# Attention over pooled image patches and text: queries and keys cut into their two parts before the turn, with the step's order rewritten on every engine

## The chip, the cores and the metric

The kernel runs on one core of one Trainium2 chip. The metric is the device time of one launch, in microseconds (us). The kernel before took 3253.87 us, the median of three runs (3253.17 to 3255.74).

## What is computed

The input is 64 images of 12 channels, 224 x 224, and 64 texts of 32 tokens, width 192. The reference, cut:

```python
pooled = x.reshape(64, 12, 14, 16, 14, 16).sum(axis=(3, 5))
h = concat([einsum('bcij,ce->bije', pooled, channel_weights), txt])  # 64 x 228 x 192
a = layernorm(h) * norm_scale + norm_bias
q, k, v = split(a @ W_attn + b_attn)        # 12 heads of 16, q and k rotated (RoPE)
att = softmax([sink, causal(q @ k.T / 4)])[..., 1:]
h = h + ((att @ v) @ W_proj + b_proj) * rezero
f = layernorm(h)                            # tokens to 8 experts, the top 2, with
h = h + moe(f)                              # capacity; rms norm, silu(g) * u, down
```

## The kernel before, in words

**Stages.** The first part of the kernel goes over the 64 images and ends with h (stored to `out`) and with every token's normed row, written to its two slots of `moe_rows` by indirect DMAs from GpSimd (L1272). The second part, from about 2040 us on, is the mixture of experts; it goes over tiles of 456 slots, adds into `out`, and is not touched by the change.

**The step.** The first part is a software pipeline of 68 steps. Five images are in work in one step, at five stages: `p` (folded and pooled), `a` (first norm, qkv product, rotation), `m` (scores for the row maxima), `t` (transposed scores, exponentials, attention, output), `z` (second norm, gate, routing, scatter). `batches` (L1188) makes the five; the image that is `p` in one step is `a` in the next. From the fifth step to the 64th, 60 steps, all five are there. Each engine has its own program, and its order inside a step is written out by hand: `step_tensor` (L1033), `step_scalar` (L1095), `step_vector` (L1134), `pass1_gpsimd` (L1229), `pass1_sync` (L1205). Semaphores join them; each engine runs strictly in its order.

**Precision.** Scores need more than one product of rounded numbers. Each query and key number is taken as a high part plus the rest, and the four 16-wide terms of a head stand side by side, so that one product of 64 rows a head gives the full score (`qk` is 114 tokens x 2 halves x 24 heads x 4 terms x 16). Before the change, GpSimd writes the rotated numbers four times over into `qk` in float32 (`add_rotation`, L713, four instructions of 768 elements a step). TensorE turns them (`turn_qk`, L880: six blocks T0 to T5 of four transposes each, L892). ScalarE copies a block into `rounded` with rounding (`round_qk`, L768, L775), and VectorE makes the parts while it moves the block to its place in `q_t` or `k_t` (`split_qk`, L538: two instructions of 64 partitions for a query block, L550; one of 128 for a key block, L556).

**Scores.** `score` (L895), nine blocks C0 to C8: C0 to C2 hold four heads of 114 x 114 (L904, L907), C3 to C8 two heads of 114 x 228 (L913, L915). VectorE takes the row maxima of each (`max_scores`, L561, L571), then `make_shift` (L573, L578) builds a tile `shift`, which TensorE turns (`turn_shift`, L919, L924), ScalarE rounds (`round_shift`, L777) and VectorE splits (`split_shift`, L583). `score_t` (L927), nine blocks S0 to S8, makes the scores of `t` again, transposed and with the shift taken off (L938 to L941, or L944 to L949). ScalarE takes their exponentials (`exp_scores`, L782), and `attend` (L953, three groups) multiplies with the values (L965, L967). `turn_y`, `normalize`, `turn_yn`, `copy_yn`, `project` (L996) and `residual` (L602) follow.

**Banks.** T, S and C blocks share PSUM banks 0 to 3 in turn, in the order of the list `RING`; `bank_free` (L864) waits for the reader of the block four places before. Bank 6 serves the channel sums, the first norm's turn, the qkv products and v in turn; bank 7 the second token half of the qk product, the turned shift, and all of z's routing.

**The norms.** `norm1_stats` on VectorE, `inverse_std` on GpSimd (L699; four small instructions, L705 to L711), `norm1_apply` on ScalarE, `turn_xn` on TensorE (L838), `copy_xn` on ScalarE, `make_qk` on TensorE (L841, one half of the tokens each), `rotate` on VectorE (L527: L533, L535) is the chain of an image at `a`.

**GpSimd's order before:** both `inverse_std`, three `fold_image` (L686), `add_rotation` 0, four scatters of z, `add_rotation` 1, `spread_patches` (L694).

**Routing.** `choose` (L615), `rank` (TensorE), `weigh` (L637), `assign` (L658). `hot_sum` (L635) adds two slices of `hot`, `seen` is added to twice (L677, L679); all four tensors there lie in SBUF, and `hot_sum` and `seen` are bf16.

Of the kernel before, what the change touches and what calls it, by code (L numbers as in the profile page):

```python
# [22 lines left out]
NG = CH // GRP  # L23
# [101 lines left out]
def build(nc, x, txt, chan_w, norm_scale, norm_bias, w_attn, b_attn, w_proj, b_proj, sinks,  # L125
# [17 lines left out]
    with ctx:  # L143
# [99 lines left out]
        gw = sb("gw", [TT, 2, 2])  # L243
        hot = sb("hot", [TT, 2, 2, E])
        hot_sum = sb("hot_sum", [TT, 2, E], bf16)
        seen = sb("seen", [TT, E], bf16)
# [63 lines left out]
        qk_rotated = [sem(f"qk_rotated{t}") for t in range(2)]  # L310
        qk_turned = [sem(f"qk_turned{k}") for k in range(6)]
        qk_rounded = sem("qk_rounded")
        qk_split = [sem(f"qk_split{k}") for k in range(6)]
# [109 lines left out]
        def setup_vector(dve):  # L423
# [12 lines left out]
            for tile in (w_qkv[C:C1, :, :], pieces[:, 0:2 * QF].bitcast(fp32), k_t[0][:, :, :, TT:TT + 1].bitcast(fp32), k_t[1][:, :, :, TT:TT + 1].bitcast(fp32),  # L436
                         shift[:, :, :], seen[:, :], val[0][:, :, :, :], val[1][:, :, :, :], row[0][:, :, :],
                         row[1][:, :, :]):
                nc.vector.memset(tile, 0.0)
# [40 lines left out]
        def setup_tensor(pe):  # L480
            pe.wait_ge(loaded, 16 * N_SMALL)
            for half in range(2):
# [9 lines left out]
        RING = [("score_t" if c == "S" else "turn", int(k)) for c, k in  # L492
                (item for item in "T0 T1 S0 T2 S1 S2 T3 S3 S4 T4 S5 S6 T5 S7 S8".split())]
        RING += [("score", k) for k in range(9)]
# [32 lines left out]
        def rotate(dve, at, t):  # L527
# [3 lines left out]
            wait(dve, qk_rotated[t], 2 * at.b)  # L531
            src = bank[6 + t][0:TT, 0:2 * D]
# [5 lines left out]
        def split_qk(dve, at, r):  # L538

            dve.wait_ge(qk_rounded, 6 * at.b + r + 1)  # L540
            src, hi = bank[bank_of("turn", r)], rounded[r % 2]
            k = TURNS[r]
            if r == 0:
                wait(dve, scored_t[8], at.b - 1)
            if k < 3:
                for side in range(2):
                    lo = slice(64 * side, 64 * side + 64)

                    dst = q_t[at.par][lo, :, :].rearrange("p (a s) n -> p a s n", s=2)[:, 2 * k:2 * k + 2, side, :]
                    ins = nc.vector.scalar_tensor_tensor(  # L550
                        out=dst, in0=hi[lo, :].bitcast(fp32).rearrange("p (a n) -> p a n", a=2), scalar=split[lo, 0:1],
                        in1=src[lo, 0:4 * TT].rearrange("p (a n) -> p a n", a=2), op0=ALU.mult, op1=ALU.add)
            else:
                kk = k - 3
                dst = k_t[at.par][:, 2 * kk:2 * kk + 2, :, 0:TT].rearrange("p a t n -> p (a t) n")
                ins = nc.vector.scalar_tensor_tensor(  # L556
                    out=dst, in0=hi[:, :].bitcast(fp32).rearrange("p (a n) -> p a n", a=4), scalar=split[:, 1:2],
                    in1=src[:, 0:4 * TT].rearrange("p (a n) -> p a n", a=4), op0=ALU.mult, op1=ALU.add)
            ins.then_inc(qk_split[r], 1)
# [55 lines left out]
        def choose(dve, at):  # L615
# [19 lines left out]
            nc.vector.tensor_tensor(hot_sum[:, :, :], hot[:, :, 0, :], hot[:, :, 1, :], ALU.add).then_inc(hots_summed, 1)  # L635

        def weigh(dve, at):  # L637

            n = at.b + 1
            dve.wait_ge(gate_exp, n)  # L640
            nc.vector.tensor_scalar(gden[:, :], gexp[:, :], 1.0, None, ALU.add).then_inc(route_step, 1)
            dve.wait_ge(route_step, ROUTE * at.b + 3)
            nc.vector.reciprocal(gw[:, :, 0:1].rearrange("p a b -> p (a b)"), gden[:, :]).then_inc(route_step, 1)
            dve.wait_ge(route_step, ROUTE * at.b + 4)
            nc.vector.tensor_tensor(gw[:, :, 1:2].rearrange("p a b -> p (a b)"), gexp[:, :],
                                    gw[:, :, 0:1].rearrange("p a b -> p (a b)"), ALU.mult).then_inc(weights_made, 1)
            dve.wait_ge(weights_made, n)
            nc.vector.tensor_tensor(wpick[:, :, :, :].rearrange("p t k e -> p (t k) e"), hot[:, :, :, :].rearrange("p t k e -> p (t k) e"),
                                    gw[:, :, :].rearrange("p t k -> p (t k)").unsqueeze(2).to_broadcast([TT, 4, E]),
                                    ALU.mult).then_inc(route_step, 1)  # L650
            dve.wait_ge(route_step, ROUTE * at.b + 5)
            nc.vector.tensor_tensor(row[at.par][:, :, COL_W:COL_W + E], wpick[:, :, 0, :], wpick[:, :, 1, :], ALU.add)
# [5 lines left out]
        def assign(dve, at):  # L658
# [5 lines left out]
            dve.wait_ge(route_step, ROUTE * at.b + 6)  # L664
            nc.vector.tensor_tensor(place, ranks, over[:, :, :], ALU.add).then_inc(route_step, 1)
            dve.wait_ge(route_step, ROUTE * at.b + 7)
            nc.vector.tensor_tensor(pick[:, :, :, :], hot[:, :, :, :],
                                    place.unsqueeze(2).to_broadcast([TT, 2, 2, E]), ALU.mult).then_inc(route_step, 1)
            dve.wait_ge(route_step, ROUTE * at.b + 8)
            nc.vector.tensor_reduce(slot_f[:, :], pick[:, :, :, :].rearrange("p t k e -> p (t k) e"), AX.X,  # L670
                                    ALU.add).then_inc(route_step, 1)
            dve.wait_ge(route_step, ROUTE * at.b + 9)
# [965 lines left out]
```

## Time and profile before

| | |
|---|---|
| median of three runs | 3253.87 us |
| the profiled execution's own time | 3250.55 us |
| span of its profile, first to last instruction | 3248.7 us |
| TensorE's granted clock, mean | 0.988 |
| busy share: TensorE, VectorE, ScalarE, GpSimd | 89%, 71%, 43%, 64% |

The profile is of one execution. A line of its views names the engine (PE is TensorE, PEld its weight loads, DVE VectorE, ACT ScalarE, POOL GpSimd), the source line, the operation, what is written and read with its size, and how often. Ends of matrix products are modelled, so the distance between starts tells more than a duration.

### The profile page before, as it was taken

How to read it: one execution, taken by the hardware profiler on the slowest of the kernel's cores; microseconds unless marked ns; L12 is line 12 of the kernel's file. 1: busy time of each engine (PE TensorE's matmuls, PEld its weight loads, DVE VectorE, ACT ScalarE, POOL GpSimd, SP SyncE). 2: the span in 40 equal slices, each digit the busy share in tenths (PEclk: the TensorE clock that was granted, in tenths of full speed). 3: DMA queues.
4: the chain of work that ended last, by engine and by line, in shares of the span. 5: the costliest groups of instructions: out<-in, count | busy, mean ns of one | idle time of the engine just before them, and what ended most of it. 6: DMA issues, size and time to landing. Idle time of an engine off the chain costs nothing.

```text
span 3248.7 us, 62759 instructions
## 1 busy us (share of the span) xinstructions
PE 2879.6 (89%) x20432; PEld 2506.3 (77%) x20432; DVE 2316.3 (71%) x5766; ACT 1393.5 (43%) x3480; POOL 2081.9 (64%) x1814
## 2 busy tenths in 40 slices
PE   2888888888888888888888886899999999999997
PEld 1777777777777777777777775899999888898987
DVE  3898898898898899889889885444544444454444
ACT  0444444444444444444444443444444444443443
POOL 2777777767777777777777763455555555555555
PEclk9999999999999999999999998999999999999999
DMA  6545544433333443443343311334344343434343
GB/s 192 161 137 146 159 142 143 137 95 93 106 104 86 106 108 81 106 108 87 99 108 95 93 49 46 63 48 69 49 69 66 50 68 47 70 47 70 47 68 45
DMA packets 205961, 297.47 MB, mean 92 GB/s; under 512 B 88375, under 2 KB 167676, under 8 KB 205875
## 3 DMA queue, kind: packets, MB, share of 16 engines
q1 hardware_dynamic: 82994, 243.82, 27.0%
q0 software_dynamic: 122880, 52.55, 11.6%
q8 instruction: 49, 0.80, 0.1%
q14 instruction: 38, 0.30, 0.0%
HBM read 201.73 MB, written 93.90 MB: 91 GB/s over the span
## 4 chain that ended last, share of the span: by engine, by line
issue 30%; POOL 29%; PE 15%; DMA 14%; DVE 7%; ACT 4%; POOLq 1%; DVEq 0%; SPq 0%; ACTq 0%
DMA out<-arena,who 13%; POOL out L1451 10%; POOL qk L723 7%; POOL moe_rows L1272 7%; POOL spread L694 3%; DVE arena L1433 3%; PE bank L847 2%; PE bank L892 2%; PE bank L965 2%; ACT xn L738 2%; POOL rstd L707 1%; PE bank L1015 1%; PE bank L838 1%; ACT prob L793 1%; PE bank L938 1%
## 5 line engine op out<-in xcount | busy, mean ns | idle before, releaser
L1451 POOL DMA_INDIRECT out<-arena,who x320 | 597.6, 1867 | 188.3 <-issue 184.1
L723 POOL TENSOR_TENSOR qk<-rot_c,rot_s 114x768 f32<-114x768 f32 x256 | 456.7, 1809 | 239.1 <-DVE rot_s L535 236.6
L1409 ACT ACTIVATE arena<-bank 128x456 f32<-128x456 f32 x320 | 174.9, 546 | 605.7 <-PE bank L1400 604.0
L1423 PE MATMUL bank<-prob,arena 128*114 128x192 f32 x2560 | 429.3, 326 | 0.0
L686 POOL TENSOR_TENSOR arena<-arena 112x896 f32<-112x896 f32 x192 | 396.5, 2095 | 44.0 <-DMA arena<-in_x 44.0
L1423 PEld LDWEIGHTS bank<-prob,arena 128*114 128x114 f32 x2560 | 412.2, 178 | 0.0
L1272 POOL DMA_INDIRECT moe_rows<-row,slot x256 | 293.3, 1146 | 99.5 <-issue 99.5
L1415 DVE TENSOR_TENSOR arena<-bank,arena 128x456 f32<-128x456 f32 x320 | 201.6, 630 | 211.8 <-ACT arena L1409 209.7
L571 DVE TENSOR_REDUCE top<-bank 114x2 f32<-114x456 f32 (+1 forms) x576 | 330.7, 620 | 1.2 <-PE bank L907 1.2
L1440 POOL TENSOR_TENSOR rms<-rms,minus_half 114x4 f32<-114x4 f32 x82 | 85.3, 1040 | 346.7 <-DVE rms L1338 346.7
L1345 DVE COPY w_slot<-arena 114x4 f32 (+1 forms) x81 | 13.8, 170 | 395.0 <-DMA out<-arena,who 395.0
L1396 PE MATMUL bank<-pieces 128*128 128x456 f32 x640 | 258.4, 404 | 26.8 <-DVE arena L1415 19.9
L550 DVE SCALAR_TENSOR_TENSOR pieces<-rounded,split,bank 64x456 fp32r<-64x456 f32 x384 | 261.5, 681 | 14.1 <-ACT rounded L775 9.3
L502 DVE TENSOR_REDUCE pooled<-arena 112x14 f32<-112x896 f32 x192 | 206.9, 1077 | 81.7 <-POOL arena L686 81.7
L790 ACT ACTIVATE prob<-bank 115x456 f32<-115x456 f32 x384 | 210.6, 549 | 86.8 <-PE bank L941 86.8
L775 ACT ACTIVATE rounded<-bank 128x456 fp32r<-128x456 f32 x384 | 210.3, 548 | 69.5 <-PE bank L892 68.5
L1400 PE MATMUL bank<-pieces 128*128 128x456 f32 x640 | 238.4, 372 | 0.0
L1398 PE MATMUL bank<-pieces 128*128 128x456 f32 x640 | 238.0, 372 | 0.0
L1399 PE MATMUL bank<-pieces 128*128 128x456 f32 x640 | 237.5, 371 | 0.0
L1397 PE MATMUL bank<-pieces 128*128 128x456 f32 x640 | 237.4, 371 | 0.0
L892 PE MATMUL bank<-ident,qk 114*128 114x114 f32 x1536 | 223.2, 268 | 5.5 <-POOL qk L723 5.5
L847 PE MATMUL bank<-w_qkv,xn_t 97*114 97x384 f32 x512 | 196.3, 507 | 21.6 <-DVE slot L674 20.8
(167 smaller groups left out, 7084.0 us busy)
## 6 DMA issues: line engine op xcount, KB each, us to landing
arena<-in_x SPq DMA_DIRECT2D x64, 2352.0 KB, 11.2
arena<-moe_rows SPq DMA_DIRECT2D x82, 363.4 KB
moe_rows<-filler SPq DMA_DIRECT2D x20, 1453.5 KB
out<-h SPq DMA_DIRECT2D x64, 171.0 KB
out<-arena,who POOLq DMA_INDIRECT x320, 5.0
arena<-in_w_t SPq DMA_DIRECT2D x9, 512.0 KB, 6.9
arena<-in_w_t SPq DMA_DIRECT2D x18, 256.0 KB, 7.3
moe_rows<-row,slot POOLq DMA_INDIRECT x256, 3.3
```

The lines of the kernel that those rows point to most:

```text
L550: ins = nc.vector.scalar_tensor_tensor(out=dst, in0=hi[lo, :].bitcast(fp32).rearrange("p (a n) -> p a n", a=2), scalar=split[lo, 0:1], in1 ...
L571: nc.vector.tensor_reduce(dst, src, AX.X, ALU.max).then_inc(maxed[k], 1)
L686: nc.gpsimd.tensor_tensor(xin[at.par][:, g, 0:mid], xin[at.par][:, g, 0:mid], xin[at.par][:, g, mid:XF], ALU.add).then_inc(x_folded, 1)
L723: nc.gpsimd.tensor_tensor(dst, a, b, ALU.add).then_inc(qk_rotated[t], 1)
L847: ins = nc.tensor.matmul(bank[6 + t][0:TT, 0:2 * D], xn_t[:, c, TT * t:TT * (t + 1)], w_qkv[:, c, 0:2 * D], start=(c == 0), stop=(c == 1))
L892: ins = nc.tensor.transpose(dst[:, TT * (2 * a + t):TT * (2 * a + t + 1)], src, ident[0:TT, 0:TT])
L1272: nc.gpsimd.indirect_dma_start(out=moe_rows[0:SLOTS, :], out_offset=bass.IndirectOffsetOnAxis(ap=slot[at.par][:, 2 * t + k:2 * t + k + 1], ...
L1396: nc.tensor.matmul(dst, hi[:, 0, col], za_hi[:, :], start=True, stop=False)
L1398: nc.tensor.matmul(dst, lo[:, 0, col], za_hi[:, :], start=False, stop=False)
L1400: ins = nc.tensor.matmul(dst, lo[:, 1, col], zb[:, :], start=False, stop=True)
L1423: ins = nc.tensor.matmul(bank[6 + s // 2][0:TT, D * (s % 2):D * (s % 2 + 1)], hid[:, j, TT * s:TT * (s + 1)], w_dn[e_par][:, j, :], start= ...
L1451: nc.gpsimd.indirect_dma_start(out=out[:, :], out_offset=bass.IndirectOffsetOnAxis(ap=who[par][:, s:s + 1], axis=0), in_=ys[par][:, s, :], ...
```

## The change

- **The parts are made before the turn.** `qk` becomes float32r. GpSimd adds the rotation in place in `rot_c` (two instructions of 192 elements per half of the tokens instead of two of 768). ScalarE writes the high parts to `qk` (`high_parts`, two of 384 elements a half), GpSimd the low ones (`low_parts`, two of 384 a half).
- **The turn** becomes a matrix product of `qk` with a float32r identity. What comes out only has to be moved: `place_q` on ScalarE (two instructions of 64 partitions a block), `place_k` on VectorE (one `tensor_copy` a block). `rounded`, `round_qk` and `split_qk` go.
- **The step's order.** The turns are done for `a` at the end of its own step, not for `m` at the start of the next. S and C blocks alternate. `turn_shift` moves from the start of the t step to the end of the m step, `project` and `residual` from the end of the t step to the start of the z step, `sum_channels` and `copy_h` from the a step to the end of the p step. Both qk products use bank 6. GpSimd's and SyncE's orders change too.
- **Routing.** `hot_sum`, the new `seen` and the weight sum are `tensor_reduce` instructions with one input; `hot_sum` and `seen` share a tile `counts` for each parity; `gw` moves to bank 7; `weigh` comes after `assign`.

```diff
-        qk = sb("qk", [TT, 2, 2 * HEADS, 4, HD])
+        qk = sb("qk", [TT, 2, 2 * HEADS, 4, HD], fp32r)
-        rounded = [sb(f"rounded{i}", [128, 4 * TT], fp32r) for i in range(2)]
-        gw = sb("gw", [TT, 2, 2])
+        gw = bank[7][0:TT, 36:40]
-                (item for item in "T0 T1 S0 T2 S1 S2 T3 S3 S4 T4 S5 S6 T5 S7 S8".split())]
-        RING += [("score", k) for k in range(9)]
+                "S0 C0 S1 C1 S2 C2 S3 C3 S4 C4 S5 C5 S6 S7 C6 S8 C7 C8 T0 T1 T2 T3 T4 T5".split()]
+        def place_q(act, at, r):
+            act.wait_ge(qk_turned[r], at.b + 1)
...
+            for side in range(2):
...
+                ins = nc.scalar.activation(dst, src[lo, 0:4 * TT].rearrange("p (a n) -> p a n", a=2), ACT.Copy)
+            ins.then_inc(qk_placed[r], 1)
+        def place_k(dve, at, r):
...
+            nc.vector.tensor_copy(dst, src).then_inc(qk_placed[r], 1)
-            nc.vector.tensor_tensor(hot_sum[:, :, :], hot[:, :, 0, :], hot[:, :, 1, :], ALU.add).then_inc(hots_summed, 1)
+                nc.vector.tensor_reduce(hot_sum[at.par], hot[:, :, :, :].rearrange("p t k e -> p t e k"), AX.X, ALU.add).then_inc(hots_summed, 1)
-            nc.vector.tensor_tensor(seen[:, :], seen[:, :], hot_sum[:, 0, :], ALU.add).then_inc(seen_counted, 1)
-            dve.wait_ge(seen_counted, 2 * at.b + 1)
-            nc.vector.tensor_tensor(seen[:, :], seen[:, :], hot_sum[:, 1, :], ALU.add).then_inc(seen_counted, 1)
+                nc.vector.tensor_reduce(seen[1 - at.par], counts[at.par][:, :, :].rearrange("p r e -> p e r"), AX.X, ALU.add).then_inc(seen_counted, 1)
         def add_rotation(pool, at, t):
...
+                ins = nc.gpsimd.tensor_tensor(c, c, sn, ALU.add)
+            ins.then_inc(qk_rotated[t], 1)
+        def low_parts(pool, at, t):
+            pool.wait_ge(qk_high[t], at.b + 1)
+            for hi, lo, of, first in piece_views(t):
+                ins = nc.gpsimd.tensor_tensor(lo, of, first.bitcast(fp32), ALU.subtract)
+            ins.then_inc(qk_low[t], 1)
+        def high_parts(act, at, t):
+            act.wait_ge(qk_rotated[t], at.b + 1)
+            wait(act, qk_turned[5], at.b)
+            for hi, lo, of, first in piece_views(t):
+                ins = nc.scalar.activation(hi, of, ACT.Copy)
+            ins.then_inc(qk_high[t], 1)
-                    ins = nc.tensor.transpose(dst[:, TT * (2 * a + t):TT * (2 * a + t + 1)], src, ident[0:TT, 0:TT])
+                    ins = nc.tensor.matmul(dst[:, TT * (2 * pair + half):TT * (2 * pair + half + 1)], src, ident_r[0:TT, 0:TT],
+                                           start=True, stop=True)
         def turn_shift(pe, at):
             pe.wait_ge(shift_made, n)
-            pe.wait_ge(qk_read[1], after(at))
+            wait(pe, routed, at.b - 1)
```

`piece_views(t)` gives, for queries and then for keys, the places of the high and of the low parts, 12 heads x 2 x 16, and the rotated numbers, read twice over. The orders inside a step after the change, with the stage of each item:

```
TensorE  S0 C0 project(z) S1 C1 S2 turn_xn(a) C2 S3 make_qk0(a) attend0(t) C3 S4 turn_xf(z)
         make_qk1(a) C4 S5 gate_logits(z) C5 S6 attend1(t) S7 C6 rank(z) S8 C7 C8 attend2(t)
         T0 T1 T2 turn_shift(m) make_v(a) turn_y(t) T3 T4 T5 sum_channels(p) turn_yn(t)
ScalarE  exp0 norm1_apply(a) exp1 exp2 copy_xn(a) exp3 norm2_apply(z) exp4 copy_xf(z)
         high_parts0(a) keep_h(m) exp5 exp_gap(z) exp6 high_parts1(a) exp7 exp8 place_q0(a)
         copy_y(t) round_shift(m) place_q2(a) copy_v(a) place_q4(a) copy_h(p) copy_yn(t)
VectorE  norm1_stats(a) max0 residual(z) norm2_stats(z) max1 max2 pool0(p) rotate0(a) max3
         pool1(p) rotate1(a) max4 max5 choose(z) max6 pool2(p) max7 max8 make_shift(m)
         assign(z) place_k1(a) split_shift(m) weigh(z) place_k3(a) normalize(t) place_k5(a)
GpSimd   inverse_std(a) fold0(p) inverse_std(z) fold1(p) add_rotation0(a) fold2(p)
         add_rotation1(a) low_parts0(a) low_parts1(a) spread_patches(p) scatter(z)
SyncE    load_image store_h2(z) load_text(p) fill_slots
```

## Rows read from the trace of the kernel before

**Rows 1.** The page, part 1: busy us, share of the span, instructions.

```profile
PE 2879.6 (89%) x20432; PEld 2506.3 (77%) x20432; DVE 2316.3 (71%) x5766; ACT 1393.5 (43%) x3480; POOL 2081.9 (64%) x1814
```

**Rows 2.** Windows, one step and the second part: PE, PEld, DVE, ACT, POOL busy; clock; DMA.

```profile
1000.50:1030.67 30.17, 26.58 (x221) 22.31 (x221) 27.00 (x66) 14.03 (x32) 21.84 (x22) 1.00 0.37 101
...
2040.00:3248.00 1208.00, 1165.25 (x6400) 1073.13 (x6400) 577.69 (x1556) 493.61 (x1477) 681.79 (x401) 0.99 0.36 58
```

**Rows 3.** Line L805, once a step, 500 to 1950 us: ns min/median/max, first and last start.

```profile
L805 ACT ACTIVATE yn_t<-bank x48: 550/551/554, 511.7 to 1929.5; 97x456 f32<-97x456 f32 x48
```

**Rows 4.** Waits of 16 steps, 1000 to 1482.7 us: in total, times, longest.

```profile
PEld bank L904 <- issue: 20.5, 16, 1.3
...
PE bank L904 <- DVE pieces L556: 17.0, 16, 1.1
...
PEld bank L838 <- ACT xn L738: 13.0, 16, 0.8
```

**Rows 5.** Timeline of TensorE in one step: start, us, line, what.

```profile
1007.16 0.44 PE L938 MATMUL bank<-pieces 128*115 128x456 f32 x1
...
1007.77 0.87 PE L1015 MATMUL bank<-gate,xf_t 96*114 96x8 f32 x8
1008.57 0.61 PE L965 MATMUL bank<-prob,val 115*32 115x228 f32 x8
...
1009.31 0.61 PE L892 MATMUL bank<-ident,qk 114*128 114x114 f32 x4
1009.68 0.44 PE L944 MATMUL bank<-mask_k,ident_r 114*114 114x456 f32 x1
...
1010.18 0.52 PE L949 MATMUL bank<-shift_t,sel 128*114 128x114 f32 x4
1010.54 1.50 PE L847 MATMUL bank<-w_qkv,xn_t 97*114 97x384 f32 x4
...
1025.81 1.47 PE L996 MATMUL bank<-w_out,yn_t 97*114 97x192 f32 x8
1027.11 1.46 PE L856 MATMUL bank<-w_qkv,xn_t 97*114 97x192 f32 x8
```

**Rows 6.** Timeline of VectorE in the same step.

```profile
1010.08 1.54 DVE L635 TENSOR_TENSOR hot_sum<-hot 114x16 bf16<-114x16 f32 x1
...
1015.82 0.19 DVE L670 TENSOR_REDUCE slot_f<-pick 114x4 f32<-114x32 f32 x1
...
1016.12 1.05 DVE L677 TENSOR_TENSOR seen<-seen,hot_sum 114x8 bf16<-114x8 bf16 x1
1017.21 1.72 DVE L679 TENSOR_TENSOR seen<-seen,hot_sum 114x8 bf16<-114x8 bf16 x1
...
1028.52 0.68 DVE L578 TENSOR_TENSOR shift<-top,sink_tok 114x48 f32<-114x48 f32 x1
```

**Rows 7.** Timeline of GpSimd in the same step.

```profile
1005.38 6.21 POOL L686 TENSOR_TENSOR arena<-arena 112x896 f32<-112x896 f32 x3
1015.35 3.56 POOL L723 TENSOR_TENSOR qk<-rot_c,rot_s 114x768 f32<-114x768 f32 x2 [3.76 <-DVE rot_s L535]
1019.11 1.20 POOL L1272 DMA_INDIRECT moe_rows<-row,slot  x1 [0.20 <-issue]
...
1024.61 3.58 POOL L723 TENSOR_TENSOR qk<-rot_c,rot_s 114x768 f32<-114x768 f32 x2
1028.14 1.47 POOL L694 TENSOR_TENSOR spread<-pooled,patch 112x196 f32<-112x196 f32 x3
```

**Rows 8.** Line L635, 1950 to 2040 us, with GpSimd nearly idle: ns min/median/max.

```profile
L635 DVE TENSOR_TENSOR hot_sum<-hot x3: 174/175/176, 1973.5 to 2016.3; 114x16 bf16<-114x16 f32 x3
```

**Rows 9.** The page, part 5: groups; busy, mean ns of one, idle before, releaser.

```profile
L571 DVE TENSOR_REDUCE top<-bank 114x2 f32<-114x456 f32 (+1 forms) x576 | 330.7, 620 | 1.2 <-PE bank L907 1.2
...
L550 DVE SCALAR_TENSOR_TENSOR pieces<-rounded,split,bank 64x456 fp32r<-64x456 f32 x384 | 261.5, 681 | 14.1 <-ACT rounded L775 9.3
```

**Rows 10.** Line L754, 500 to 1950 us: a copy of 384 elements in SBUF on ScalarE.

```profile
L754 ACT ACTIVATE h_keep<-h x49: 514/514/515, 500.4 to 1948.2; 114x384 f32<-114x384 f32 x49
```

More of the change, by code:

```diff
@@ L536, in rotate @@
                                     sin[:, t, :].unsqueeze(1).to_broadcast([TT, 24, 16]), ALU.mult).then_inc(qk_read[t], 1)
-        def split_qk(dve, at, r):
-            dve.wait_ge(qk_rounded, 6 * at.b + r + 1)
-            src, hi = bank[bank_of("turn", r)], rounded[r % 2]
+        def place_q(act, at, r):
+            act.wait_ge(qk_turned[r], at.b + 1)
+            if r == 0:
+                wait(act, scored_t[8], at.b - 1)
             k = TURNS[r]
-            if r == 0:
-                wait(dve, scored_t[8], at.b - 1)
[L545 to L559, printed above, removed]
@@ L634, in choose @@
             wait(dve, seen_counted, at.b)
-            nc.vector.tensor_tensor(hot_sum[:, :, :], hot[:, :, 0, :], hot[:, :, 1, :], ALU.add).then_inc(hots_summed, 1)
+            with nc.allow_low_precision(reason="whole numbers up to 128"):
+                nc.vector.tensor_reduce(hot_sum[at.par], hot[:, :, :, :].rearrange("p t k e -> p t e k"), AX.X, ALU.add).then_inc(hots_summed, 1)
         def weigh(dve, at):
             n = at.b + 1
+            first, second = (gw.rearrange("p (t k) -> p t k", t=2)[:, :, i] for i in range(2))
@@ L880, in turn_qk @@
-        def turn_qk(pe, at, last, r):
-            n = at.b + 1
+            for stages in (now, last_step):
+                while at >= 0:
+                    kind, k = RING[at]
+                    held_by = stages[kind]
+                    if held_by:
+                        freed = {"turn": qk_placed, "score": maxed, "score_t": probed}[kind][k]
+                        return pe.wait_ge(freed, held_by.b + 1)
+                    at -= 4
+                at += len(RING)
+        def turn_qk(pe, a, m, t, r):
+            n = a.b + 1
@@ L1022, in rank @@
             pe.wait_ge(hots_summed, n)
-            wait(pe, seen_counted, 2 * at.b)
+            wait(pe, seen_counted, at.b)
             first, second = bank[7][0:TT, 0:E], bank[7][0:TT, E:2 * E]
-            nc.tensor.matmul(first, before[:, :], hot_sum[:, 0, :], start=True, stop=False)
-            nc.tensor.matmul(first, ones[:, :], seen[:, :], start=False, stop=True)
-            nc.tensor.matmul(second, before[:, :], hot_sum[:, 1, :], start=True, stop=False)
-            nc.tensor.matmul(second, ones[:, :], hot_sum[:, 0, :], start=False, stop=False)
@@ L1029, in rank @@
-            nc.tensor.matmul(second, ones[:, :], seen[:, :], start=False, stop=True).then_inc(ranks_made, 1)
+            nc.tensor.matmul(first, before[:, :], hot_sum[at.par][:, 0, :], start=True, stop=False)
+            nc.tensor.matmul(first, ones[:, :], seen[at.par], start=False, stop=True)
+            nc.tensor.matmul(second, before[:, :], hot_sum[at.par][:, 1, :], start=True, stop=False)
+            nc.tensor.matmul(second, ones[:, :], hot_sum[at.par][:, 0, :], start=False, stop=False)
@@ L1033, in step_tensor, with ring @@
+            nc.tensor.matmul(second, ones[:, :], seen[at.par], start=False, stop=True).then_inc(ranks_made, 1)
         def step_tensor(pe, p, a, m, t, z):
-            def half1(items):
+            def ring(items):
                 for c, k in items.split():
-                    if c == "T" and m:
-                        turn_qk(pe, m, t, int(k))
-                    elif c == "S" and t:
-                        score_t(pe, t, m, int(k))
-            half1("T0")
-            if t:
-                turn_shift(pe, t)
@@ L1151, in step_vector @@
+            if a:
+                rotate(dve, a, 1)
+            maxima("4 5")
             if z:
                 choose(dve, z)
+            maxima("6")
+            if p:
+                pool_image(dve, p, 2)
+            maxima("7 8")
             if m:
-                split_qk(dve, m, 4)
+                make_shift(dve, m)
+            if z:
+                assign(dve, z)
+            if a:
+                place_k(dve, a, 1)
+            if m:
+                split_shift(dve, m)
             if z:
```

359 lines of the change are left out of this document (171 added, 188 removed).

## The prediction

> **What bounds the kernel now.** I read the page first: TensorE is busy 89% of the span [rows 1]. The windows split that [rows 2]: the second part, 1208 us, is nearly full and untouched, so its time stays. One step of the first part takes 30.17 us; (1929.5 - 511.7) / 47 between the first and last start of a once-a-step line gives the same [rows 3]. In it VectorE is busy 27.0 us, TensorE 26.6, GpSimd 21.8, ScalarE 14.0. Nobody is full: each runs in its written order and waits in turn. The waits of 16 steps show where TensorE loses [rows 4]: 1.28 us a step (20.5 / 16) ahead of a score block, nearly all of it until VectorE has split a key block, and pieces of 0.8 elsewhere.
>
> **TensorE's own work** I take from distances between starts [rows 5]: an S block of two heads 0.61 us (six), one of four 0.86 (three), an attend 0.74 (three), a turn 0.37 (six), the gate 0.80, a qk product at most 1.5, I take 1.4 (two), project and v 1.30 each (eight products), so the twelve of the channel sums 1.95. C blocks have no row here: C0 to C2 are built like S blocks, 0.61; C3 to C8 have three products instead of four, 0.45. Together 3.7 + 2.6 + 2.2 + 2.2 + 0.8 + 2.8 + 2.6 + 1.95 + 1.8 + 2.7 = 23.4; the small turns and the rank add 2.3 at the turn's 0.09 a transpose: 25.7 us. So about 4.5 us of each step is waiting, and 25.7 is the floor after the change too, if the turn costs the same.
>
> **Part by part.**
> - *Turn as a product.* Four float32r products of 114 columns take 0.36 us (from 1010.18 to 1010.54), four float32 transposes 0.37 [rows 5]: nothing gained or lost. The Trainium skill ("Perfetto Trace Analysis", Transposes) says to use a transpose, not a standard matmul, for a turn; that speaks against the change, but here the row shows no difference.
> - *VectorE.* Six query and three key splits go, each about 0.68 [rows 9]: -6.1. Three `place_k` come, PSUM to SBUF, 128 x 456: not below 0.5, not above the split's 0.68; I take 0.6: +1.8. `hot_sum` takes 1.54 and the two `seen` 1.05 and 1.72 [rows 6]. They are waits: the first starts at 1010.08 and ends at 1011.62, GpSimd's folds end at 1011.59; the others end with GpSimd's two additions (1015.35 + 3.56) [rows 6, 7]. With GpSimd idle `hot_sum` takes 0.174 [rows 8]. The Trainium skill ("SBUF — State Buffer", SBUF: two separate sides) has this rule: a VectorE operation with two SBUF inputs and a GpSimd one that reads SBUF exclude each other for a whole instruction. The trace agrees. As reductions with one input they should take 0.19, as the reduction at 1015.82 does next to a running GpSimd instruction [rows 6]: -3.9. VectorE: 27.0 - 6.1 + 1.8 - 3.9 = 18.8 us. `make_shift` keeps two SBUF inputs and stays at 0.68.
> - *ScalarE.* Six roundings of 0.55 become six placements of about 0.55: even. Four high parts of 384 elements at 0.51 [rows 10] are new; with scattered writes at most 0.68: +2.1. About 16 us, not a bound.
> - *GpSimd.* Four instructions of 768 elements (1.8 each, 7.1) go [rows 7]. New are four of 192 and four of 384. `spread` does 196 in about 0.5, and the slope between 196 and 768 is 2.3 ns an element: 0.5 and 0.94, together 5.8. The lower bound is 0.5 for each (4.0), the upper one 1.8 for each (14.2). I take 5.8: the size is nearest `spread`. GpSimd: 20.4.
> - *SyncE.* The store of z moves ahead of the text load. It waits for `residual`, now early in the step; the text is needed a step later. Nothing, unless z's chain is late by most of a step.
> - *Fill and drain.* The same 68 steps; project only changes side of a boundary. Zero, give or take 10 us.
>
> **The new step, in order of time** (0 = S0 on TensorE). S0 C0 project S1 C1 S2 end at 4.6. `turn_xn` needs the norm: `copy_h` ended at the boundary, `norm1_stats` 1.3, then GpSimd. But GpSimd still scatters z of the step before, which it began only after `weigh`, near the step's end: four scatters span 5.5 us (1019.11 to 1024.6) [rows 7] and end at about 2.7. Inverse std 1.5, apply 1.0: 5.3. TensorE waits 0.7. Then C2 S3 qk0 attend0 C3 S4 qk1 to 12, C4 S5 gate C5 S6 attend1 S7 C6 rank to 17.3, S8 C7 C8 19.0, attend2 19.8. On GpSimd std, fold0 6.3, std, fold1 9.9, rotation0 10.9, fold2 13, rotation1 14, low parts 15.9 and 17.8: T0 at 19.8 has 2.0 us to spare. T0 to T2 end at 20.9. `turn_shift` waits for `assign`: C8 19.1, maxima 19.8, `make_shift` 20.5, five small ones 21.5: TensorE waits 0.7. Then turn_shift, v, turn_y, T3 to T5, channel sums, turn_yn: 21.6 + 0.2 + 1.3 + 0.6 + 1.1 + 1.95 + 0.4 = 27.1, the floor and two waits of 0.7. Next to it `round_shift`, `split_shift`, `weigh` end at 24.2, the scatters at 29.8, which is 2.7 of the next step: the two loops close at about the same length. Banks, maxima and exponentials fit between alternating S and C blocks (each pair 1.06 to 1.3 us, a maximum 0.62, an exponential 0.55) [rows 9]. **27.1 us a step**; the delays of semaphores lie in the distances between starts.
>
> **The sum.** 60 full steps x (30.17 - 27.1) = 184 us. The profiled execution took 3250.55 us (1.85 around its span), 0.1% under the median of 3253.87; I set the change against the median: 3070 us.
>
> **Rivals.**
> - *A: the GpSimd loop is longer than my sketch.* Scatter, inverse std, `turn_xn`, the step, `assign`, `weigh`, scatter is a closed loop now, and what is late in it is late one for one; ScalarE's and VectorE's `exp1` and `max4` stand behind `norm1_apply` and `rotate1`. For: both ends meet at 2.7 without slack, and low parts have only 2.0. Against: VectorE has 8 us free. A step of 28.5 gives 3254 - 100 = 3154.
> - *B: the waits vanish.* If scatters and routing are quicker than read, TensorE runs at its floor, 25.7: 3254 - 268 = 2986. Against: `turn_shift` must wait for the maxima.
> - *C, slower: the parts on GpSimd hold the turn.* T0 waits for the second low parts. At the upper bound, 1.8 each, eight instructions take 14.4 instead of 5.8; they end at 26.4, T0 is 6.6 late, a step is 33.7: +212 us, 3466. It is slower than before once T0 is over 3.1 late, that is with the eight over 5.8 + 2.0 + 3.1 = 10.9 us, 1.4 each. For: `first` and the repeated operand are strided, and a part waits for ScalarE's high part. Against: the instructions replaced are strided too.
> - *D, slower: the turn as a dear product.* The rule on transposes would give this. At the pace of `project` (1.30 us for four float32 products, 0.33 each) 24 of them take 7.8 instead of 2.2 on the fullest engine: a step of 32.7, 3254 + 152 = 3406. Against: the 0.36 of the float32r products.
> - *E: no change.* VectorE's relief would go entirely into new waits.
>
> **How the numbers follow.** My forecast (26.2 to 28) 0.55; A (28 to 30) 0.22; B 0.10; C 0.08; D 0.03; E 0.02. Predicted: 3070. The low end is a step of 25.8, 3254 - 262 = 2992, nearly B; the high end one of 29.0, 3254 - 70 = 3184. Left out are C, D, E, the end of A and the bottom of B, 0.2 together. A measurement tells about 0.2% from no change. Faster 0.87, same 0.02, slower 0.11.
>
> **What the profile after should show.** The once-a-step line about 27.1 us apart; VectorE busy near 19 us a step, ScalarE 16, GpSimd 20, TensorE as before; `hot_sum` and `seen` 0.2 us each beside a working GpSimd; low parts under 1.0; a turn block 0.37; waits of TensorE at `turn_xn` for ScalarE and at `turn_shift` for VectorE, each below 1 us, none at T0. I am wrong if T0 waits for GpSimd, if inverse std starts late enough for TensorE to wait over 2 us at `turn_xn`, or if the second part moves.

## The result, and the profile after

The kernel after takes 3112.28 us, the median of four runs (3110.01 to 3120.22), against 3254.8 us before (four runs, 3253.17 to 3258.36): a ratio of 0.9565, with a 95% interval of 0.9546 to 0.9584. It is 142 us faster, where 184 were forecast: right in direction, 42 us off in size, inside the range. The profiled execution took 3111.47 us with a span of 3109.3 us, 139.4 less than the span before.

The page after, part 1 (busy us, share of the span, instructions; compare [rows 1]) and part 5 (the turn and its new helpers; busy, mean ns of one, idle before, releaser):

```profile
PE 2852.4 (92%) x20432; PEld 2539.9 (82%) x20432; DVE 1827.3 (59%) x5319; ACT 1497.5 (48%) x3736; POOL 2019.5 (65%) x2070
...
L725 POOL TENSOR_TENSOR qk<-rot_c,qk 114x384 fp32r<-114x384 f32 x256 | 253.7, 1014 | 44.4 <-ACT qk L746 44.4
L547 ACT ACTIVATE pieces<-bank 64x456 fp32r<-64x456 f32 x384 | 209.2, 545 | 149.3 <-PE bank L905 147.1
L905 PE MATMUL bank<-ident_r,qk 114*128 114x114 f32 x1536 | 202.2, 282 | 9.7 <-POOL qk L725 9.7
L905 PEld LDWEIGHTS bank<-ident_r,qk 114*128 114x128 f32 x1536 | 186.5, 196 | 22.1 <-POOL qk L725 19.6
```

VectorE is 489 us less busy, TensorE 27. In a full step VectorE was relieved of 8 us, and the step, as the next paragraph shows, fell by 2.5: something else closes it now.

**Where the 139.4 us came from.** The once-a-step line of `norm1_apply` (L738 before, L761 after) starts 64 times. Its first start is at 61.2 us before and 61.57 after. The next three distances, in which the pipeline fills, sum to 69.6 before (21.76, 21.34, 26.49) and to 85.8 after (30.96, 31.09, 23.74): 16.2 us lost. The 60 distances behind them have a mean of 30.17 before and 27.65 after: 151 us gained. What comes behind the last of them takes 4.8 us less. Full steps thus gained 151 of the 184 that I forecast, and the fill, which I had put at nothing, gave 16 of it back.

Two windows of after, each as long as one step and starting some 0.35 us behind S0 (PE, PEld, DVE, ACT, POOL busy; clock; DMA; compare [rows 2]):

```profile
1003.20:1030.10 26.90, 25.50 (x221) 22.42 (x220) 18.88 (x58) 15.52 (x37) 20.66 (x27) 1.00 0.40 104
1030.10:1059.50 29.40, 27.20 (x221) 22.88 (x220) 19.40 (x58) 15.61 (x37) 21.22 (x27) 0.94 0.41 108
```

The same 221 products take 1.7 us longer in the second window, and the granted clock there is 0.94. Steps come in two kinds: most are 27.2 to 27.4 us long (the distance between starts of `turn_xn` or of `norm1_apply`), and 11 of the 60 are longer, ten of them by some 1.6 us and one, early on, by 3.0. I call the others clean. Clean steps average 27.3 us; the long ones add (10 x 1.6 + 3.0) / 60 = 0.3. (From S0 to S0 the first window's step is only 26.9 us, because the `turn_xn` behind it waits 0.5 us longer than its own.)

Waits of 16 steps of after, 1000 to 1444.8 us (in total, times, longest; compare [rows 4]):

```profile
POOL moe_rows L1281 <- issue: 86.8, 67, 4.3
ACT xn L761 <- POOL shifted L710: 58.9, 16, 4.0
...
PEld bank L852 <- ACT xn L761: 26.5, 16, 2.0
PE bank L852 <- ACT xn L761: 24.3, 16, 1.9
...
PE bank L938 <- DVE slot L674: 3.6, 11, 0.4
```

TensorE's one large wait is at `turn_xn`, 24.3 / 16 = 1.5 us a step; it is 1.3 to 1.5 in some steps and 1.8 to 1.9 in others. The wait at `turn_shift` (L938) is 0.2, and T0 doesn't wait. The first row says why `turn_xn` is late: GpSimd stands over 4 us a step before the scatters, until `row` is there. Timeline of GpSimd in after (start, us, line, what, idle before):

```profile
1000.67 1.20 POOL L1281 DMA_INDIRECT moe_rows<-row,slot  x1 [4.26 <-issue]
1002.17 1.13 POOL L1281 DMA_INDIRECT moe_rows<-row,slot  x1 [0.30 <-issue]
...
1005.04 1.12 POOL L1281 DMA_INDIRECT moe_rows<-row,slot  x1 [0.30 <-issue]
1006.17 0.22 POOL L704 TENSOR_TENSOR var<-mv,ln_eps 114x2 f32<-114x2 f32 x1
...
1007.55 0.19 POOL L710 TENSOR_TENSOR shifted<-zeros,scaled 114x2 f32<-114x2 f32 x1
...
1022.20 1.53 POOL L693 TENSOR_TENSOR spread<-pooled,patch 112x196 f32<-112x196 f32 x3
1027.87 1.20 POOL L1281 DMA_INDIRECT moe_rows<-row,slot  x1 [4.14 <-issue]
```

And VectorE's in the same step:

```profile
1004.29 0.25 DVE L518 BATCH_NORM_AGGREGATE mv<-st 114x2 f32<-114x6 f32 x2 [0.16 <-DVE st L514]
...
1019.39 0.19 DVE L635 TENSOR_REDUCE counts<-hot 114x16 bf16<-114x32 f32 x1
...
1022.66 0.21 DVE L577 TENSOR_TENSOR shift<-top,sink_tok 114x48 f32<-114x48 f32 x1
...
1026.65 0.16 DVE L653 CAST row<-token 114x2 uint32<-114x2 f32 x1
```

The statistics of `a` are ready at 1004.54, but GpSimd takes them up at 1006.17, when its last scatter is issued. TensorE has done all ahead of `turn_xn` at 1007.46 and starts it at 1008.82. At the far end GpSimd is free from 1023.73 on, `row` is whole at 1026.81, and the first scatter starts at 1027.87.

### The profile page after: what moved, and what is told of

The parts are those of the page before. It is cut to its first block, busy times and chain, and to the rows that moved or that the text cites. A ratio compares the mean times of both kernels' runs of the same rounds, so it can differ in the third digit from the quotient of the medians.

```text
span 3109.3 us, 62400 instructions
## 1 busy us (share of the span) xinstructions
PE 2852.4 (92%) x20432; PEld 2539.9 (82%) x20432; DVE 1827.3 (59%) x5319; ACT 1497.5 (48%) x3736; POOL 2019.5 (65%) x2070
## 3 DMA queue, kind: packets, MB, share of 16 engines
q1 hardware_dynamic: 82994, 243.82, 27.4%
## 4 chain that ended last, share of the span: by engine, by line
PE 32%; issue 22%; POOL 19%; DMA 14%; DVE 6%; ACT 4%; POOLq 1%; DVEq 1%; SPq 0%; ACTq 0%
DMA out<-arena,who 13%; POOL out L1460 10%; PE bank L861 6%; POOL moe_rows L1281 5%; PE bank L979 3%; PE bank L927 3%; DVE arena L1442 3%; PE bank L952 2%; PE bank L954 2%; PE bank L905 2%; PE bank L1029 2%; POOL rstd L706 2%; PE bank L963 1%; PE bank L852 1%; PE bank L929 1%
## 5 line engine op out<-in xcount | busy, mean ns | idle before, releaser
L570 DVE TENSOR_REDUCE top<-bank 114x2 f32<-114x456 f32 (+1 forms) x576 | 352.9, 622 | 240.9 <-PE bank L921 153.4
L1449 POOL TENSOR_TENSOR rms<-rms,minus_half 114x4 f32<-114x4 f32 x82 | 85.3, 1040 | 345.3 <-DVE rms L1347 345.3
L725 POOL TENSOR_TENSOR qk<-rot_c,qk 114x384 fp32r<-114x384 f32 x256 | 253.7, 1014 | 44.4 <-ACT qk L746 44.4
L547 ACT ACTIVATE pieces<-bank 64x456 fp32r<-64x456 f32 x384 | 209.2, 545 | 149.3 <-PE bank L905 147.1
L1405 PE MATMUL bank<-pieces 128*128 128x456 f32 x640 | 258.7, 404 | 23.9 <-DVE arena L1424 16.7
L905 PE MATMUL bank<-ident_r,qk 114*128 114x114 f32 x1536 | 202.2, 282 | 9.7 <-POOL qk L725 9.7
L905 PEld LDWEIGHTS bank<-ident_r,qk 114*128 114x128 f32 x1536 | 186.5, 196 | 22.1 <-POOL qk L725 19.6
```

The source lines that it names most:

```text
L570: nc.vector.tensor_reduce(dst, src, AX.X, ALU.max).then_inc(maxed[k], 1)
L725: ins = nc.gpsimd.tensor_tensor(lo, of, first.bitcast(fp32), ALU.subtract)
L905: ins = nc.tensor.matmul(dst[:, TT * (2 * pair + half):TT * (2 * pair + half + 1)], src, ident_r[0:TT, 0:TT], start=True, stop=True)
L1405: nc.tensor.matmul(dst, hi[:, 0, col], za_hi[:, :], start=True, stop=False)
```

## The experiments

Each undoes or adds one thing, on the kernel after unless it says the one before. Nothing of the computation is left out in any of them; two add products that nobody reads. The times of the kernel before beside them were 3254 to 3256 us.

**1. Weigh first.** `weigh` stands directly behind `assign`; the weights get a tile of their own in SBUF.

```diff
-        gw = bank[7][0:TT, 36:40]
+        gw_t = sb("gw", [TT, 4])
+        gw = gw_t[:, :]
...
                 assign(dve, z)
+                weigh(dve, z)
...
                 split_shift(dve, m)
-            if z:
-                weigh(dve, z)
```

> weigh comes right after assign on VectorE, ahead of place_k1 and split_shift, and its weights lie in SBUF again. Theory 1 (the loop weigh, scatters, inverse std, norm1_apply, turn_xn holds TensorE): the row is whole about 1.7 us earlier in the step, the scatters begin that much earlier, TensorE's wait at turn_xn (1.5 us a step on average) falls under 0.3 us, and the steps in which the clock falls behind that wait go too. A step goes from 27.65 to about 26.1 us, the time from 3112 to about 3020. Rival (TensorE's own work and the wait for assign at turn_shift set the step): the wait at turn_xn only moves to another place, the time stays within 10 us of 3112.

Measured: 2992.95 us, ratio 0.92 (0.9185 to 0.9216), 119 us under the kernel after and 27 less than I expected. The full step is 25.66 us (25.31 to 26.19), the fill that of the kernel after (86.1 for 85.8). Waits of 1000 to 1400 us in this kernel:

```profile
POOL moe_rows L1281 <- issue: 52.8, 62, 2.7
...
ACT xn L762 <- POOL shifted L711: 24.9, 15, 2.0
```

GpSimd stands 52.8 us (in 400) instead of 86.8 (in 445), and TensorE's products wait at `turn_xn` no more; two of its weight loads do, 0.6 us in all. TensorE is busy 396 of the 400 us, at a clock of 1.00. `row` is whole 1.00 us after the last instruction of `assign` (1010.12 to 1011.12), where it was 2.91 in the kernel after (1023.90 to 1026.81), and the step is 1.99 shorter. Their place, behind a key block and a wait for ScalarE, is what made the seven small instructions of `weigh` dear.

**2. The scatters a step later.** Image z's scatters are issued in the step after its own, when their rows have long been there: the same loop is cut in another place.

```diff
+                done = Batch(half, par, 5) if known is None or 0 <= known - 5 < B else None
...
-                if z:
-                    scatter_waits(pool, z, fill)
+                if done:
+                    scatter_waits(pool, done, fill)
...
-            for i in range(B, B + 4):
+            for i in range(B, B + 5):
```

> The scatters of an image are issued one step later, at the same place of GpSimd's order, so GpSimd never waits for weigh; VectorE's order is that of the changed kernel. Theory 1 (the loop weigh, scatters, inverse std, turn_xn): the loop is open, the wait at turn_xn goes, a step goes from 27.65 to TensorE's own 25.5 to 25.8 us, 2985 to 3000, as in the run with weigh first. Rival (weigh first helped by something else in VectorE's order, its place against place_k or the weights' tile): the step stays near 27.6 and the time near 3110.

Measured: 3006.43 us, ratio 0.923 (0.9214 to 0.9246), the full step 25.74. The weights' tile and VectorE's order are those of the kernel after here, so it is the loop that gives the gain, and nothing else in experiment 1's edit. With the wait for the row gone instead of shortened, the step is that of experiment 1 within 0.1 us. The profiled execution takes 13 us more than experiment 1's behind the last step (1316.0 against 1303.2); that wasn't taken apart.

**3. Products in place of the wait.** Seven products stand ahead of `turn_xn`, so that TensorE works where it waited.

```diff
+            if z:
+                for _ in range(7):
+                    nc.tensor.matmul(bank[4][0:TT, 0:4 * TT], ident_r[0:TT, 0:TT], mask_q0[:, :, :], start=True, stop=True)
             if a:
                 turn_xn(pe, a)
```

> Seven extra products of 456 columns, with a result that nobody reads, fill TensorE's wait ahead of turn_xn; nothing else is changed. If the steps of 29 us (11 of the 60) come from the clock that falls to its lower level behind that wait: they go, the granted clock stays at 1.00 in the steady steps, and the time falls by 11 x 2 = 22 us less what the filler costs where the wait is shorter than its 1.5 us, 3090 to 3105. If the long steps come from elsewhere (a late transfer, GpSimd): they stay, and the time is 3112 or up to 15 us more.

Measured: 3102.2 us, ratio 0.9531 (0.9515 to 0.9547). One long step is left, the first; the other 59 are 27.2 to 27.5, and the mean is 27.36. The 60 steps give 17 us; in the profiled execution 12 of them are lost behind the last step, where the second part shows a clock of 0.99 and 0.98 against 1.00 and 0.99 (2100 to 2500 us, and from 2500 us to the end). So work that does nothing makes the kernel faster, and the long steps are the clock's.

**4. The turn as a transpose.**

```diff
-                    ins = nc.tensor.matmul(dst[...], src, ident_r[0:TT, 0:TT],
-                                           start=True, stop=True)
+                    ins = nc.tensor.transpose(dst[...], src.bitcast(fp32),
+                                              ident[0:TT, 0:TT])
```

> The turn is made of float32 transposes again, of the same parts. A block of four takes 0.37 us instead of the 0.45 to 0.50 that the product takes in the changed kernel, so TensorE has 0.5 to 0.7 us less to do in a step. If TensorE's work sets the step: 0.6 x 60 = 36 us less, about 3076. If the loop through GpSimd sets it (theory 1): T0 to T2 stand ahead of a wait for assign and outside that loop, and nearly nothing is gained, 3105 to 3112. The Trainium skill (Perfetto Trace Analysis, Transposes) prefers the transpose for a turn; its rule gives the first outcome in sign, not in size.

Measured: 3088.17 us, ratio 0.9492 (0.9476 to 0.9507), 24 us under the kernel after, between the two outcomes expected: 8 in the fill (77.9), 17 in the steps (27.37). Clean steps didn't change; two long ones are left of eleven, both at the very end. Why transposes should be followed by fewer falls of the clock, no run shows. Timeline of TensorE in the fill, first the kernel after:

```profile
77.48 2.81 PE L905 MATMUL bank<-ident_r,qk 114*128 114x114 f32 x12 [6.17 <-POOL qk L725]
...
82.50 2.90 PE L905 MATMUL bank<-ident_r,qk 114*128 114x114 f32 x12
85.19 4.07 PE L843 MATMUL bank<-chan,spread 112*114 112x192 f32 x12
```

Then the kernel with transposes:

```profile
77.34 2.54 PE L905 MATMUL bank<-ident,qk 114*128 114x114 f32 x12 [6.16 <-POOL qk L725]
...
81.89 1.33 PE L905 MATMUL bank<-ident,qk 114*128 114x114 f32 x12
83.06 2.12 PE L843 MATMUL bank<-chan,spread 112*114 112x192 f32 x12
```

Both start at half their pace, at which TensorE was already ahead of this wait (in the kernel after, the qk product at 68.44 us takes 2.88 us instead of 1.46). With transposes the full pace is back at the second three blocks; with products it isn't even for the channel sums, which take 4.07 us instead of 2.1. This is where most of the fill's 8 us come from. TensorE's clock records in the two traces begin, at the upper level, at 81.5 us with transposes and at 89.1 with products, 7.6 us later; half of that is 3.8, and the first distance of the fill is 3.9 shorter (27.01 for 30.95). The next stretch at the lower level lasts 20.5 us instead of 27.3, and the second distance is 3.6 shorter. In a full step the same twelve take 1.39 and 1.33 us as transposes. As products they take more, in this timeline of TensorE in a clean step of after:

```profile
1006.94 0.52 PE L963 MATMUL bank<-shift_t,sel 128*114 128x114 f32 x4
1008.82 0.63 PE L852 MATMUL bank<-ident,xn 114*97 114x114 f32 x4 [1.36 <-ACT xn L761]
...
1010.42 1.46 PE L861 MATMUL bank<-w_qkv,xn_t 97*114 97x384 f32 x4
...
1022.45 1.55 PE L905 MATMUL bank<-ident_r,qk 114*128 114x114 f32 x12
1023.96 0.39 PE L938 MATMUL bank<-ident,shift 114*128 114x114 f32 x2
...
1026.06 1.53 PE L905 MATMUL bank<-ident_r,qk 114*128 114x114 f32 x12
1027.42 2.16 PE L843 MATMUL bank<-chan,spread 112*114 112x192 f32 x12
```

From start to start the two threes take 1.51 and 1.36 us. The difference from the transposes, 1.55 + 1.53 - 1.39 - 1.33 = 0.36 us a step, is hidden as long as `turn_xn` waits for GpSimd anyway. Now a long step of after:

```profile
1036.17 0.63 PE L852 MATMUL bank<-ident,xn 114*97 114x114 f32 x4 [1.84 <-ACT xn L761]
...
1037.78 2.57 PE L861 MATMUL bank<-w_qkv,xn_t 97*114 97x384 f32 x4
1040.28 1.01 PE L979 MATMUL bank<-prob,val 115*32 115x228 f32 x8
```

The same qk product takes 2.57 us instead of 1.46 and the attend 1.01 instead of 0.61: for some three microseconds, from 1.6 us behind the wait's end, TensorE works at the lower of its two levels (1.2 instead of 2.4 GHz).

**5. The reductions on the kernel before.** Its order stays as it was; `hot_sum` and `seen` become reductions with one input, so that VectorE no longer meets GpSimd there.

```diff
-            nc.vector.tensor_tensor(hot_sum[:, :, :], hot[:, :, 0, :], hot[:, :, 1, :], ALU.add).then_inc(hots_summed, 1)
+            nc.vector.tensor_reduce(hot_sum[at.par], hot[...].rearrange("p t k e -> p t e k"), AX.X, ALU.add).then_inc(hots_summed, 1)
...
-            nc.vector.tensor_tensor(seen[:, :], seen[:, :], hot_sum[:, 0, :], ALU.add).then_inc(seen_counted, 1)
-            dve.wait_ge(seen_counted, 2 * at.b + 1)
-            nc.vector.tensor_tensor(seen[:, :], seen[:, :], hot_sum[:, 1, :], ALU.add).then_inc(seen_counted, 1)
+            nc.vector.tensor_reduce(seen[1 - at.par], counts[at.par][...].rearrange("p r e -> p e r"), AX.X, ALU.add).then_inc(seen_counted, 1)
```

> The kernel before with only the routing sums changed: hot_sum and seen by reductions with one input, in a tile per parity. The three take 0.2 us each instead of 4.3 us together. If those waits were on the path before the change (the score block C1 waited for a key block that stood behind seen): TensorE's 1.3 us at the second score block goes and hot_sum no longer delays rank and T4, a step of about 28.7 us, 3254 - 90 = 3165, so most of the change's gain. If VectorE's time only hid other waits (loops through ScalarE, the order of blocks): at most 20 us less, 3235 or more.

(`hot_sum` and `seen` share a tile `counts` for each parity, as in the change.) Measured: 3265.21 us, ratio 1.0035 (1.0021 to 1.0049): 11 us slower than the kernel before beside it, though the three routing sums take 3.8 us a step less. VectorE's busy time in one step falls by only 2.1 us (24.88 against 27.00 [rows 2]), because `make_shift` meets GpSimd now: it takes 2.20 us instead of 0.68 [rows 6]. Rows of GpSimd and VectorE in this kernel:

```profile
998.25 3.58 POOL L723 TENSOR_TENSOR qk<-rot_c,rot_s 114x768 f32<-114x768 f32 x2
...
1000.65 2.20 DVE L578 TENSOR_TENSOR shift<-top,sink_tok 114x48 f32<-114x48 f32 x1
```

A row of TensorE's timeline:

```profile
1063.21 0.61 PE L892 MATMUL bank<-ident,qk 114*128 114x114 f32 x4 [1.15 <-POOL qk L723]
```

And its waits from 1000 to 1480 us:

```profile
PE bank L892 <- POOL qk L723: 19.7, 16, 1.3
```

T0 now waits for GpSimd's rotated numbers, 1.2 us in every step, a wait that the kernel before doesn't have. The granted clock in 1000 to 1400 us is 0.94 (1.00 in [rows 2]) and most steps are 30.68 long; the few clean ones are 29.1 to 29.3.

**6. The same, with the clock held.** Six products at the start of the step are added to experiment 5.

```diff
+            if z:
+                for _ in range(6):
+                    nc.tensor.matmul(bank[4][0:TT, 0:4 * TT], ident_r[0:TT, 0:TT], mask_q0[:, :, :], start=True, stop=True)
             half1("T0")
```

> The kernel before with the reductions in the routing, and six products of 456 columns whose result nobody reads at the start of each step, where TensorE now waits for GpSimd's last rotation. If most steps of that kernel are 30.7 instead of 29.1 us because the clock falls behind the wait: all come to 29.1 or a little more, the granted clock is 1.00, the time goes from 3265 to 3175 to 3195. If the long steps have another cause, they stay: 3265 or more.

Measured: 3199.26 us, ratio 0.9833 (0.9818 to 0.9848), a step of 29.24, clock 1.00. 60 x (30.17 - 29.24) = 56 us: ending VectorE's waits at the routing sums is worth that much in the old order, with `make_shift` still waiting (2.2 us), but only with TensorE kept at its upper level.

**7. The additions back in the kernel after.**

```diff
-                nc.vector.tensor_reduce(hot_sum[at.par], hot[...].rearrange("p t k e -> p t e k"), AX.X, ALU.add).then_inc(hots_summed, 1)
+            nc.vector.tensor_tensor(hot_sum[at.par], hot[:, :, 0, :], hot[:, :, 1, :], ALU.add).then_inc(hots_summed, 1)
...
-                nc.vector.tensor_reduce(seen[1 - at.par], counts[at.par][...].rearrange("p r e -> p e r"), AX.X, ALU.add).then_inc(seen_counted, 1)
+            nc.vector.tensor_tensor(seen[1 - at.par], seen[at.par], hot_sum[at.par][:, 0, :], ALU.add).then_inc(seen_counted, 1)
+            dve.wait_ge(seen_counted, 2 * at.b + 1)
+            nc.vector.tensor_tensor(seen[1 - at.par], seen[1 - at.par], hot_sum[at.par][:, 1, :], ALU.add).then_inc(seen_counted, 1)
```

> The changed kernel with hot_sum and seen as additions of two SBUF inputs again. hot_sum meets GpSimd's low parts, the seen additions its low parts or spread, and each waits for the end of a GpSimd instruction, at most 1.0 us each. They stand ahead of place_k1, split_shift and weigh, so in the loop of theory 1: weigh is 0.5 to 2.5 us later and a step longer by that, 3140 to 3260. Rival (VectorE has 8 us free in a step, its waits are hidden): within 10 us of 3112.

Measured: 3116.67 us, ratio 0.9563 (0.9542 to 0.9585), not to be told from the kernel after. Line L634 of this kernel, from 500 to 1700 us (ns min/median/max):

```profile
L634 DVE TENSOR_TENSOR counts<-hot x43: 174/177/188, 520.6 to 1681.9; 114x16 bf16<-114x16 f32 x43
```

The addition that took 1.54 us before [rows 6] takes 0.18 in the new order, as in [rows 8], and the two of `seen` take 0.15 and 0.16. `hot_sum` starts less than 0.2 us before the end of a low part, behind which GpSimd waits for the next high part, and the two of `seen` fall where GpSimd waits for the row. In the new order the reductions are worth nothing.

**8. Better versions.** Four combinations, to see what bounds the step once `weigh` is early. First, experiments 1 and 4 together:

> Both: weigh straight after assign, and the turn by float32 transposes. With weigh first TensorE is busy 99% of a step of 25.66 us, so its own work is the bound now and the cheaper turn, worth nothing in the undisturbed steps before, should count in full: 0.6 us a step and 8 us in the first steps, a step of 25.1, about 2950. If a loop stands right behind (GpSimd's, with the scatters ending just in time): 2975 to 2990, from the first steps alone.

Measured: 2989.05 us, ratio 0.9183 (0.9167 to 0.92): a miss of 39. The fill gives its 9 us (76.8), the step stays at 25.68. The three blocks are shorter, but `turn_shift` waits for `assign` instead, as this row of TensorE's timeline shows:

```profile
1004.58 0.39 PE L939 MATMUL bank<-ident,shift 114*128 114x114 f32 x2 [0.51 <-DVE slot L675]
```

Second, the channel sums and `copy_h` ahead of T3 to T5 in the steps of the fill (the diff shows TensorE's part):

```diff
+            if p and not t:
+                sum_channels(pe, p)
             ring("T3 T4 T5")
-            if p:
+            if p and t:
                 sum_channels(pe, p)
```

> As the run before it in this call, and in the steps that have no image at t yet the channel sums of p come ahead of T3 to T5. The first three steps are one chain through the channel sums; three blocks (2.8 us at the lower clock) leave it in each: 6 to 9 us less than that run. If the first steps are bound elsewhere (the folds, the image loads): no difference.

Measured: 2992.29 us, ratio 0.9191 (0.9176 to 0.9207), the fill 78.1: no gain, so I take it that the channel sums' place isn't what makes the fill long.

Third, the first combination with `assign` ahead of the last two maxima, and `weigh` behind `make_shift`:

```diff
+            if z:
+                assign(dve, z)
             maxima("7 8")
             if m:
                 make_shift(dve, m)
             if z:
-                assign(dve, z)
+                weigh(dve, z)
```

> Weigh first and transposes, and assign ahead of max7 and max8 on VectorE, with weigh after make_shift. If what is left of TensorE's waiting is the 0.5 us at turn_shift for assign, which took what the transposes gave: it goes, and a step falls from 25.68 to 25.1 to 25.3 us, 2955 to 2970. Rival (max7 and max8, now 1.1 us later, hold T2 and turn_shift as much as assign did, or GpSimd's loop is next): a step stays at 25.7, 2985 or more.

Measured: 2968.73 us, ratio 0.9126 (0.9114 to 0.9139): the fastest, 144 us under the kernel after. The step is 25.40 us (25.28 to 25.82). Its window of 400 us:

```profile
1000.00:1400.00 400.00, 397.36 (x3459) 346.17 (x3459) 299.35 (x913) 244.68 (x550) 330.85 (x413) 1.00 0.43 115
```

Fourth, the same without transposes:

> As the run before it, with the turn as the product of the changed kernel. If TensorE's own work is now the only bound, the dear turn shows in full: 0.33 + 0.18 us a step, the differences of two groups of three blocks, and about 9 us in the first steps, so 35 to 45 us above that run. If other waits still cover it: the first steps alone, 5 to 10 us above.

Measured: 2976.58 us, ratio 0.9145 (0.9132 to 0.9157): 8 us, all in the fill (86.3 against 77.7); the step is 25.43. I had expected the turn's full price, since TensorE is now the bound. The products take more of TensorE's time, and the step is as long; what else closes it at 25.4 is open.

## Why the forecast was right and where it failed

**Right.** The change shortened the step, and VectorE fell from 27.0 to 18.9 us a step as worked out (18.8), ScalarE came to 15.5 (16), GpSimd to 20.7 (20.4). A low part takes 1.01 us (0.94), a place of q 0.545 (0.55), of k 0.62 (0.6). T0 doesn't wait in a full step, so rival C fell, and the turn is a little dearer as a product but not by D's price; from the last full step on the time is 4.8 us less. TensorE's floor of 25.7 was near: experiments 1 and 2 reach 25.66 and 25.74, which is rival B's step. It is no floor, though, since experiment 8 reaches 25.40, and 25.43 with the dearer turn; the sum of TensorE's work was at least 0.3 too high.

**The step that failed: four scatters that "end at about 2.7", so that "TensorE waits 0.7".** The loop of `weigh`, scatters, inverse std and `turn_xn` was in the sketch, but mis-sized, and not its small instructions: counted from S0, `row` was whole at 23.9 (24.2 forecast), the scatters span 5.5, inverse std 1.5. I let the first scatter start as soon as `row` is whole. It starts 1.06 us later (1026.81 to 1027.87; in experiment 1 the distance is 1.05), a delay that no row of before showed, since there the scatters stand behind GpSimd's own additions [rows 7]. In experiment 2, where the row is long there, the first scatter starts 0.2 us behind `spread`. So they end at 3.3, `turn_xn` starts at 5.95, and TensorE, ready at 4.6, waits 1.5 on average instead of 0.7. The other wait I named, 0.7 at `turn_shift`, is 0.2: T2 ended at 21.1 instead of 20.9, and the slots were whole at 20.9 instead of 21.5 in the step shown, where `make_shift` took 0.21 us, not 0.68. (It takes 0.21 in 19 of the 60 steps and about 0.6 in the others.) The two errors partly cancel, so that the small loss in clean steps is in part luck: they came to 27.33 for 27.1, 14 us. This is rival A's mechanism, with a small price. Experiments 1 and 2 cut the loop at two places, and each gives 1.9 to 2.0 us a step: the wait's 1.5, the long steps' 0.3 and, in experiment 1, 0.1 at `turn_shift`.

**What the sum left out: the clock.** I priced a wait at its length. Behind this one the granted clock falls in 11 of 60 steps: 10 x 1.6 + 3.0 = 19 us. Experiment 3 takes the falls away and leaves the wait; experiment 4 takes most of them.

**Fill and drain: "Zero, give or take 10 us".** The fill costs 16. Before, an image's turns belonged to the next step; now its chain from statistics to turns and the next image's channel sums lie in one step, with long waits in between while few images are there, and TensorE at half pace behind them. Experiment 4 gives 8 of it back. The other 8 weren't taken apart; a part is again the clock, since with transposes it is at the lower level from 88.4 to 108.8 us, and in the kernel before only from 75.1 to 78.5 and from 85.3 to 88.8.

14 + 19 + 16 = 49 us of loss, less 4 from the rest of the span: 45, as many as the profiled execution misses (184 - 139.4); by the medians 42 are missing.

**The turn's price.** I took 0.37 a block from products with 114 columns [rows 5]; those of `turn_qk` load 128 columns and take 1.51 and 1.36 us for three blocks, 0.45 to 0.50 each. The row I read was near, but not the same. The Trainium skill ("Perfetto Trace Analysis", Transposes) says to turn with a transpose; the runs agree in sign, by 24 us in the kernel after and 8 in the best one, though by the clock and the fill and not by a full step.

**The lock.** The Trainium skill ("SBUF — State Buffer", SBUF: two separate sides) has the rule that made me take 3.9 us off VectorE. Rows and runs agree with it (1.54 us against 0.18), but experiments 5 to 7 show that this is not where the change's gain lies: alone it makes the old order 11 us slower, and in the new order it is worth nothing. The rule also bears on `make_shift`, which keeps two SBUF inputs: it took 2.2 us in experiment 5, 0.68 before, and 0.21 where it doesn't wait. What is left for the gain is the new order and the parts made before the turn; no run separates these two.

## What to carry to other kernels

Look for the loop that closes over the step's boundary, and follow it through every engine, down to the one that only issues DMAs: a consumer's short wait was set by seven small instructions standing in the wrong place on an engine with 8 us to spare. Put first what feeds such a loop. A wait of TensorE isn't worth its length alone; where the clock falls behind it, it costs twice, and relieving another engine can make a kernel slower by creating one.

## What the runs showed of the hardware

- Whether the clock falls isn't told by the wait's length alone. In the kernel after, of 43 steps between 500 and 1672 us, the 22 waits of 1.31 to 1.36 us at `turn_xn` were never followed by a long step; of the 21 waits of 1.44 to 1.91 six were. With transposes, 43 waits of 1.44 to 1.98 in the same stretch were followed by none, and then one of 1.96 at 1723.7 us by a step of 30.29. What decides is open.
- The first indirect DMA on GpSimd starts 1.06 us after the instruction that completes the row it sends (1.01 to 1.20 over the 64 images, and 1.01 to 1.21 in experiment 1), though its slots have been there for 4 us and GpSimd idle as long; the next ones follow every 1.43 us (1.13 and 0.30).
- The granted clock of a window means something only where the trace has a record of the clock. In the kernel after these records begin at 89.1 us. The window of 74 to 92 us prints 1.00, though the turns and channel sums in it are at half pace (2.90 and 4.07 us at 82 and 85 us). From there on record and pace agree:

```profile
92.50:119.80 27.30, 22.32 (x79) 18.82 (x80) 11.68 (x19) 7.82 (x16) 13.65 (x14) 0.50 0.41 140
```
